# GIN's first layer: where each edge's row goes, ranked in two passes over the source bins, and 17 instead of 14 turns of row scatters inside the GIN stage

## The chip, the cores and the metric

The kernel runs on one core of one Trainium2 chip. The metric is the device time of one execution in microseconds; lower is better. The engines are TensorE (PE in the rows, its weight loads PEld), VectorE (DVE), ScalarE (ACT), GpSimd (POOL) and the DMA queues, of which SP is one.

## The reference, cut to what matters

The whole kernel is four graph layers in a row on one graph of 3125 nodes and 53125 edges, each followed by a residual and a normalisation: a GIN, an edge MLP, a GENConv and an interaction layer. Only the GIN's first of four rounds is touched:

```
for l in range(4):
    S = segment_sum(X[src], dst, 3125)
    Z = (1 + eps[l]) * X + S
    h = relu(bn(Z @ W1[l].T + b1[l]))
    h = relu(bn(h @ W2[l].T + b2[l]))
    X = h @ W3[l].T + b3[l]
```

The interaction layer at the end wants the edges sorted by source, where the input has them sorted by destination. So, beside the GIN, the kernel works out for each edge its place in the order by source, and scatters the edge's row of 24 words there in device memory.

## The kernel before, in words

The stages follow each other with a barrier of all engines between them: `prepare`, `adjacency` (the dense 3125 x 3125 count matrix `adj`, in fp16 in SBUF), `gin`, a normalisation, `edge_mlp`, another, `genconv`, `interaction`. A barrier waits for every engine, SP and GpSimd included.

In `gin` the aggregation of a round is a product of `parts` (the node features times W1, split into three bf16 parts, 97 columns) with `adj`, for 25 tiles of nodes (slots) and seven column pieces of at most 450 (`PIECES`), each piece in a PSUM bank of its own (banks 0 to 6). Bank 7 is what is left.

The places are worked out in the first round, between those products. An edge lies at row p and column c of a 125 x 425 table, in order of destination. Its bin h (0 to 24) is its source node divided by 125, `bins` in float32. For each bin h:

- VectorE marks the edges of the bin: `hots(h)`, L663.
- TensorE counts with two matmuls, L847 and L848, into 426 columns: edges of the bin above in the same column, and in the column before.
- ScalarE copies the counts from PSUM: `bin_steps`, L795.
- VectorE runs a scan along the columns, L671, that starts at the end of the bin before, so that the result is the edge's place in the whole order; it then picks out the edges of the bin, L678, into `chosen[h % 2]`.
- GpSimd adds `chosen` to `places_f`, L640.

The first four bins come before everything else of the round, in banks 5 and 6; then follow the small joined weights (L859 to L867), the node features (L883), and the product, with one bin counted in bank 7 after each slot from the fourth on. The remaining 21 bins stand on VectorE behind the bounds and weights of the later rounds (L753 to L762). ScalarE and VectorE copy the finished pieces out (L816, L773) after the last bin has been added. VectorE then turns places into rows (L776 to L780), and SP writes `deg_row` (L615) and `places` (L617), loads the edges' rows (`pay`) and places in sets of four columns, and GpSimd scatters each column with one indirect DMA (L646): `GIN_TURNS` = 14 turns of 8, so 112 of the 425 columns. `gin` ends when SP has seen them all land. The other 313 columns are scattered in `genconv` (L1631): EACH = (53 - GIN_TURNS) // 3 turns of 8 in each of its three rounds, and what is left behind the last. At the head of each such round GpSimd has a reduction (L1636) on which VectorE waits, behind the scatters of the round before.

Of the kernel before, what the change touches and what calls it, by code (L numbers as in the profile page):

```python
# [7 lines left out]
ALU = mybir.AluOpType  # L8
# [42 lines left out]
GIN_TURNS = 14  # L51
EARLY_BINS, FIRST_TILE = 4, 3
# [43 lines left out]
def build(nc, a, out):  # L96
    ctx = ExitStack()
    with ctx, nc.allow_non_contiguous_dma(reason="small columns"):
# [40 lines left out]
        ranks = dict(bins=apart(P, NC), places_f=apart(P, NC), place_i=apart(P, NC, I32), before=apart(P, P, BF16), upto=apart(P, P, BF16))  # L139
# [20 lines left out]
def prepare(G, keep, ranks):  # L160
# [3 lines left out]
    hi, before, rest = (ranks[k] for k in ("bins", "before", "upto"))  # L164
# [16 lines left out]
    raw_s, of_bin = hi.bitcast(I32), w_(P, NC)  # L181
# [9 lines left out]
    with nc.Block() as block:  # L191
# [10 lines left out]
        def _(eng):  # L202
            imprecise = dict(allow_small_or_imprecise_dtypes=True)
            step = Steps(eng, s_p)
            for out, size in ((lo, 0), (up, 1)):
# [5 lines left out]
            eng.memset(ident[:, :], 0.0)  # L211
            eng.memset(rest, 1.0).then_inc(s_const, 1)
# [5 lines left out]
                              pattern=[[1, P]], channel_multiplier=-1)  # L218

            eng.affine_select(out=rest, in_=rest, compare_op=ALU.is_ge, fill=0.0, base=0,  # L220
                              pattern=[[-1, P]], channel_multiplier=1).then_inc(s_const, 1)
# [35 lines left out]
        def _(eng):  # L257
# [40 lines left out]
            eng.tensor_copy(hi, of_bin)  # L298
# [38 lines left out]
def adjacency(G, keep):  # L337
# [3 lines left out]
    nc, sem, work, ps, adj_all, adj, over_d = (  # L341
        G[k] for k in ("nc", "sem", "work", "ps", "adj_all", "adj", "over_d"))
    key_v, low_v, key_c, low_c, over_n, over = (keep[k] for k in (
        "key_v", "low_v", "key_c", "low_c", "over_n", "over"))
    w_ = Words(work, 0, KEPT)
# [4 lines left out]
    code, base_w, low_iota = w_(P, WCOLS, I16), w_(P, NW), w_(P, P * F, BF16)  # L350
    low_wv = w_(P, NW * F, BF16)
    low3 = low_wv.rearrange("p (w v) -> p w v", v=F)
    iota3 = low_iota.rearrange("p (c v) -> p c v", v=F)
    low_x, code_x = w_(P, P, BF16), w_(P, WCOLS, BF16)
    code16, far, one, key_neg = w_(P, WCOLS, F16), [w_(P, WCOLS, F16) for _ in range(2)], w_(P, 1), w_(P, NW)
# [12 lines left out]
    s_low = sem("remainders_turned")  # L368
# [128 lines left out]
def gin(G, ranks):  # L497
# [50 lines left out]
    one_row = Words(G["extra"], 1536)(1, D)  # L548
    blank = T[1][:, zeroed:t_.at]
    X, S = T[1], T[2]  # L550
    bins, places_f, place_i, before, upto = (ranks[k] for k in ("bins", "places_f", "place_i", "before", "upto"))
    r_ = Words(T[2])
    total, steps, chosen = ([r_(P, n) for _ in range(2)] for n in (NC + 1, NC + 1, NC))
    hot = [r_(P, NC + 2, BF16) for _ in range(2)]
    RANK = [(6, 5)[h % 2] if h < EARLY_BINS else 7 for h in range(NT)]
    assert FIRST_TILE + NT - EARLY_BINS < NT
# [17 lines left out]
    def within_group(g, c0, c1):  # L574
# [3 lines left out]
    s_load, s_x_in, s_zero, s_merge, s_v = (sem(n) for n in ("weights_loaded", "x_loaded", "weights_zeroed", "merge_ready",  # L578
                                                             "vector_step"))
# [8 lines left out]
    s_clear, s_hot, s_rank, s_steps, s_scan = (sem(n) for n in (  # L588
        "ranks_cleared", "bin_hot", "bin_counted", "bin_read_out", "bin_scanned"))
# [3 lines left out]
    with nc.Block() as block:  # L593
        @block.sync
        def _(eng):
            eng.dma_start(T[0], a["x"]).then_inc(s_x_in, 16)
# [32 lines left out]
        def _(eng):  # L629
            eng.memset(blank, 0.0).then_inc(s_zero, 1)  # L630
# [5 lines left out]
            for u in range(NT):  # L636
                eng.wait_ge(s_chosen, u + 1)
                if u:
                    eng.wait_ge(s_placed, u)
                eng.tensor_tensor(places_f, places_f, chosen[u % 2], ALU.add).then_inc(s_placed, 1)  # L640
# [9 lines left out]
        def _(eng):  # L650
# [3 lines left out]
            for k in range(2):  # L654
                eng.memset(hot[k][:, 0:1], 0.0)
                eng.memset(hot[k][:, NC + 1:NC + 2], 0.0).then_inc(s_clear, 1)
            eng.memset(total[1][:, NC:NC + 1], 0.0).then_inc(s_clear, 1)

            def hots(h):

                if h >= 2:
                    eng.wait_ge(s_rank, h - 1)
                eng.tensor_scalar(hot[h % 2][:, 1:NC + 1], bins, float(h), None, ALU.is_equal).then_inc(s_hot, 1)  # L663

            def place_bin(h):
                eng.wait_ge(s_steps, h + 1)
                if h:
                    eng.wait_ge(s_chosen, h)
                else:
                    eng.wait_ge(s_clear, 3)  # L670
# [4 lines left out]
                eng.wait_ge(s_scan, h + 1)  # L675
                if h >= 2:
                    eng.wait_ge(s_placed, h - 1)
                eng.scalar_tensor_tensor(chosen[h % 2], bins, float(h), total[h % 2][:, 0:NC], ALU.is_equal,  # L678
                                         ALU.mult).then_inc(s_chosen, 1)

            hots(0)
            hots(1)
            for u in range(EARLY_BINS):
                place_bin(u)
# [20 lines left out]
            eng.scalar_tensor_tensor(abs_b, abs_b, -1.0, abs_b, ALU.mult, ALU.max).then_inc(s_limits, 1)  # L705
            step(eng.tensor_scalar(w1e[:, 3 * GH:4 * GH], w1, eps[:, 0:1], None, ALU.mult))
# [32 lines left out]
            for l in range(GL):  # L739
# [11 lines left out]
                if l == 0:  # L751
                    eng.wait_ge(s_bound, 1)
# [11 lines left out]
                    for u in range(EARLY_BINS, NT):  # L764
                        place_bin(u)
                    eng.wait_ge(s_placed, NT)
                for i, j in enumerate(DVE_P):
# [6 lines left out]
                if l == 0:  # L774
                    whole, part = places_f, place_i.bitcast(F32)
                    step(eng.tensor_scalar(part, whole, 1.0 / EW, 0.5 / EW - 0.5, ALU.mult, ALU.add))  # L776
                    step(eng.tensor_scalar(part, part, MAGIC, -MAGIC, ALU.add, ALU.add))
                    step(eng.scalar_tensor_tensor(whole, part, -float(EW), whole, ALU.mult, ALU.add))
                    step(eng.scalar_tensor_tensor(whole, whole, float(PAIR * PAIRS), part, ALU.mult, ALU.add))
                    eng.tensor_copy(place_i, whole).then_inc(s_places, 1)  # L780
# [9 lines left out]
        def _(eng):  # L790
            def bin_steps(h):
                eng.wait_ge(s_rank, h + 1)
                if h >= 2:
                    eng.wait_ge(s_scan, h - 1)
                eng.activation(steps[h % 2], ps[0:P, RANK[h], 0:NC + 1], ACT.Copy).then_inc(s_steps, 1)  # L795

            for u in range(EARLY_BINS):
                bin_steps(u)
            eng.wait_ge(s_load, 208)
            for l in range(GL):  # L800
# [5 lines left out]
                if l == 0:  # L806
                    for u in range(EARLY_BINS, NT):
                        bin_steps(u)
                    eng.wait_ge(s_placed, NT)
# [26 lines left out]
        def _(eng):  # L836
            def bin_counts(h):
                eng.wait_ge(s_clear, 2)
                eng.wait_ge(s_hot, h + 1)
                for k in range(h):  # L840
                    if RANK[k] == RANK[h]:
                        free = k
# [1729 lines left out]
```

## Time and profile before

| what | us |
|---|---|
| median of three runs | 2290.88 (2289.26 to 2296.27) |
| the profiled execution, own time | 2297.08 |
| its span, first to last instruction | 2295.4 |
| mean granted TensorE clock | 0.781 of full speed |
| PE / PEld / DVE / ACT / POOL busy | 81% / 58% / 60% / 50% / 59% of the span |

All start times are microseconds from the span's start in the one profiled execution. The profiled execution was 6.2 us slower than the median of the three timed ones. Busy shares of the whole span say little here, since each stage has a limit of its own: the stage `gin` is what counts.

### The profile page before, as it was taken

To read this page: it belongs to the slowest core of one execution; us is meant where nothing else is said; L and a number is where in the kernel's file an instruction comes from. 1 tells how busy PE (TensorE), PEld (TensorE's weight loads), DVE (VectorE), ACT (ScalarE), POOL (GpSimd) and SP (SyncE) were. 2 spreads that over 40 slices of the span, in tenths; PEclk is the share of its full clock that TensorE was granted. 3 is DMA by queue.
4 is the path that set the end of the run, shared out by engine and by line. 5 is a ranking of instruction groups with operands and counts; after the bars stand their busy time and mean duration, and the time that the engine had idled before them with its cause. 6 is when DMAs were issued, how large, how long until landed. Compare 5 with 4: busy or idle time off the path is not lost. (4 is left out here: it accounts for less than half of the span.)

```text
span 2295.4 us, 42015 instructions
## 1 busy us (share of the span) xinstructions
PE 1867.0 (81%) x8353; PEld 1331.7 (58%) x8353; DVE 1371.3 (60%) x4158; ACT 1154.8 (50%) x2623; POOL 1361.8 (59%) x1337
## 2 busy tenths in 40 slices
PE   3888578776898989999889989989986667777677
PEld 2666444445788878888555545545564445555454
DVE  6999592224444444444266577567457777777775
ACT  2999112221566666666253073073135666666663
POOL 1000136772677777777147778878727777777771
PEclk9999697877555565555679999999987777777767
DMA  0000101112444444444111111111232222222221
GB/s 12 0 0 0 45 1 19 18 18 64 106 119 117 117 119 121 119 117 119 57 40 18 19 17 17 20 17 18 40 130 64 64 65 65 64 65 65 65 63 37
DMA packets 195684, 128.61 MB, mean 56 GB/s; under 512 B 138365, under 2 KB 177854, under 8 KB 194587
## 3 DMA queue, kind: packets, MB, share of 16 engines
q0 software_dynamic: 40256, 60.21, 12.2%
q1 hardware_dynamic: 151388, 58.11, 10.1%
q10 hardware_dynamic: 3841, 8.16, 1.0%
q8 instruction: 62, 1.02, 0.2%
q14 instruction: 137, 1.12, 0.2%
HBM read 106.83 MB, written 13.34 MB: 52 GB/s over the span
## 5 line engine op out<-in xcount | busy, mean ns | idle before, releaser
L2204 POOL DMA_INDIRECT adj<-h_rows,adj x416 | 395.5, 951 | 155.9 <-issue 76.5
L1255 POOL DMA_INDIRECT work<-p_rows,small x416 | 394.9, 949 | 126.7 <-issue 101.7
L1631 POOL DMA_INDIRECT edge_rows<-pay,small x313 | 383.0, 1224 | 98.1 <-issue 92.8
L2421 PE MATMUL ps<-adj 128*128 128x125 f32 x928 | 210.9, 365 | 157.7 <-DVE adj L2299 154.1
L1439 PE MATMUL ps<-work 128*128 x1024 | 298.4, 445 | 43.4 <-ACT work L1375 40.6
L2421 PEld LDWEIGHTS ps<-adj 128*128 128x128 f32 x928 | 174.4, 259 | 253.5 <-issue 160.3
L1439 PEld LDWEIGHTS ps<-work 128*128 128x128 f32 x1024 | 231.9, 314 | 66.7 <-issue 59.9
L1332 DVE TENSOR_TENSOR work<-ps,work 128x256 f32<-128x256 f32 x256 | 108.7, 425 | 250.3 <-PE ps L1439 140.2
L1450 PE MATMUL ps<-small,work 128*128 128x64 f32 x1024 | 244.2, 392 | 11.2 <-DVE small L1321 8.0
L1450 PEld LDWEIGHTS ps<-small,work 128*128 128x128 f32 x1024 | 239.0, 321 | 21.7 <-DVE small L1321 17.5
L1993 PE MATMUL ps<-adj,work 125*128 (+2 forms) x1008 | 206.0, 361 | 20.5 <-DVE work L1722 20.5
L1993 PE MATMUL ps<-adj,extra 125*128 (+2 forms) x1092 | 214.8, 352 | 0.0
L486 PE MATMUL ps<-work 125*125 125x500 bf16 x628 | 162.8, 402 | 38.6 <-DVE work L417 38.6
L2411 PE MATMUL ps<-adj 112*128 112x256 f32 x464 | 188.5, 498 | 1.0 <-ACT adj L2344 1.0
L2289 DVE SCALAR_TENSOR_TENSOR adj<-adj 128x128 f32<-128x128 f32 x464 | 144.1, 350 | 65.8 <-POOLq L2209 52.9
L1993 PEld LDWEIGHTS ps<-adj,work 125*128 (+1 forms) x1008 | 100.3, 99 | 119.3 <-issue 29.2
L1372 ACT ACTIVATE work<-work 64x256 f32<-64x256 int32 x256 | 128.4, 502 | 76.6 <-DMA work<-edge_attr 52.9
L1993 PEld LDWEIGHTS ps<-adj,extra 125*128 (+1 forms) x1092 | 106.3, 97 | 101.7 <-issue 0.8
L486 PEld LDWEIGHTS ps<-work 125*125 125x125 bf16 x628 | 114.6, 192 | 86.9 <-DVE work L417 62.2
L1383 ACT ACTIVATE work<-work 128x256 f32<-128x256 f32 x256 | 105.8, 413 | 110.5 <-DVE work L1332 105.4
L646 POOL DMA_INDIRECT edge_rows<-pay,small x112 | 133.3, 1190 | 45.6 <-issue 44.7
L417 DVE TENSOR_SCALAR work<-work 125x500 bf16<-125x500 int16 x549 | 153.5, 401 | 0.0
(417 smaller groups left out, 3111.8 us busy)
## 6 DMA issues: line engine op xcount, KB each, us to landing
work<-dst_all SPq DMA_DIRECT2D x256, 64.0 KB
work<-edge_attr SPq DMA_DIRECT2D x256, 64.0 KB
edge_rows<-pay,small POOLq DMA_INDIRECT x425, 2.7
work<-p_rows,small POOLq DMA_INDIRECT x416
adj<-h_rows,adj POOLq DMA_INDIRECT x416
adj<-adj SPq DMA_DIRECT2D x232, 24.0 KB
pay<-edge_pay SPq DMA_DIRECT2D x106, 46.9 KB
adj<-edge_rows ACTq DMA_DIRECT2D x1, 2496.0 KB, 10.0
```

Of the source, the lines that this page charges most:

```text
L417: eng.tensor_scalar(ring[k][v], code, key_v[:, at], None, ALU.is_equal).then_inc(s_code, 1)
L486: eng.matmul(ps[0:P, parity * WG + k, 0:WCOLS], lows[k][:, v, :], ring[k][v], start=v == 0, stop=v == F - 1).then_inc(s_used, 1)
L646: eng.indirect_dma_start(edge_rows[:, :], bass.IndirectOffsetOnAxis(ap=place[:, k:k + 1], axis=0), pay[:, k * ROW:(k + 1) * ROW], None).th ...
L1255: eng.indirect_dma_start(gathered[:, at:at + D], None, p_rows[:, :], bass.IndirectOffsetOnAxis(ap=src_i[:, c:c + 1], axis=0)).then_inc(s_g ...
L1439: ins = eng.matmul(PROD[v % 2][:, k * D:(k + 1) * D], kmat[b][:, k * EW:(k + 1) * EW], qw[:, bass.ds(w * D, D)], start=True, stop=True)
L1450: ins = eng.matmul(SUM[v % 2], rows[v % 2][:, k * D:(k + 1) * D], hot[v % 2][:, k * MW:(k + 1) * MW], start=k == 0, stop=k == PAIR - 1)
L1631: eng.indirect_dma_start(edge_rows[:, :], bass.IndirectOffsetOnAxis(ap=place[:, k:k + 1], axis=0), pay[:, k * ROW:(k + 1) * ROW], None).th ...
L1993: ins = eng.matmul(ps[:, j, 0:cw], part_of(p, s), cols, start=first, stop=last, skip_group_check=True)
L2204: eng.indirect_dma_start(gathered[:, at:at + D], None, h_rows[:, :], bass.IndirectOffsetOnAxis(ap=row3_i[:, c, DST_C:DST_C + 1], axis=0)). ...
L2289: ins = eng.scalar_tensor_tensor(msg[b][:, k * D:(k + 1) * D], soft[b][:, k * D:(k + 1) * D], rows_t[:, bass.ds((c + k) * ROW + RCUT_C, 1) ...
L2411: eng.matmul(PROD[v % DEPTH], attr_t[f % 2], w_f[:, cols], start=True, stop=True).then_inc(s_prod, 1)
L2421: ins = eng.matmul(SUM[v % 2], msg[b][:, k * D:(k + 1) * D], hot[b][:, k * P:(k + 1) * P], start=k == 0, stop=k == PAIR - 1)
```

## The change

- **Two passes.** The ranks are made in two passes over the bins. Pass one: 25 marks, and one matmul each, that adds the count of every column for each bin into one PSUM tile `TOTAL` (25 x 425). VectorE copies it and runs one scan per bin row (all 25 at once); one small matmul gives each bin's start (`BASE`); four more VectorE instructions give offsets, split in a high and a low bf16 part. Pass two: 25 marks again, and three matmuls per bin (counts above in the column, and the two parts of the bin's offset row) straight into a rank in PSUM. The scan per bin and ScalarE's copy are gone; VectorE multiplies mark and rank out of PSUM. `bins` is bf16.
- **Banks and order.** The ranks use banks 5 and 6 in turn, so the product runs over pieces 0 to 4 for all 25 slots first, with the rank of the next slot's bin before each; pieces 5 and 6 follow for all 25 slots after the last bin has been chosen. Five bins (`EARLY`) are placed ahead of the later rounds' bounds and weights, the other twenty behind them. The matmuls of the bounds move behind the first half of the node features.
- **Rows.** VectorE turns places into rows before it copies the pieces out. SP's list is the same: it waits for all copies, writes `deg_row`, then `places`.
- **x.** The load of x moves from the head of `gin` to the head of `adjacency`, whose buffers make room for it.
- **Scatters.** `GIN_TURNS` is 17: 136 columns in `gin`, 289 in `genconv` (EACH is 12).

```diff
-GIN_TURNS = 14
-EARLY_BINS, FIRST_TILE = 4, 3
+GIN_TURNS = 17
...
+            eng.dma_start(T[0], a["x"]).then_inc(s_x_in, 16)
+            eng.wait_ge(s_x_in, 16)
...
             def place_bin(h):
-                eng.wait_ge(s_steps, h + 1)
...
-                eng.tensor_tensor_scan(total[h % 2], steps[h % 2], steps[h % 2], total[1 - h % 2][:, NC:NC + 1],
-                                       ALU.add, ALU.max).then_inc(s_scan, 1)
                 if h + 2 < NT:
-                    hots(h + 2)
...
+                    hots(NT + h + 2)
+                if h >= 3:
+                    eng.wait_ge(s_placed, h - 2)
+                eng.wait_ge(s_rank, h + 1)
+                eng.scalar_tensor_tensor(chosen[h % 3], bins, float(h), RANK[h], ALU.is_equal,
                                          ALU.mult).then_inc(s_chosen, 1)
...
+            for n in range(NT):
+                hots(n)
+            eng.wait_ge(s_count, NT)
+            step(eng.tensor_copy(off, TOTAL))
+            step(eng.tensor_tensor_scan(upto, off, off, 0.0, ALU.add, ALU.max))
...
+            for u in range(NT):
+                eng.wait_ge(s_hot, u + 1)
+                eng.matmul(TOTAL, mark[:, NT - 1 - u:2 * NT - 1 - u], hot[u % 4], start=u == 0,
+                           stop=u == NT - 1).then_inc(s_count, 1)
...
+            def rank(h):
+                eng.wait_ge(s_hot, NT + h + 1)
+                if h >= 2:
+                    eng.wait_ge(s_chosen, h - 1)
+                at = ident16[:, h:h + 1].to_broadcast([NT, P])
+                eng.matmul(RANK[h], before, hot[(NT + h) % 4], start=True, stop=False)
+                eng.matmul(RANK[h], at, off_high, start=False, stop=False)
+                eng.matmul(RANK[h], at, off_low, start=False, stop=True).then_inc(s_rank, 1)
...
+                    eng.wait_ge(s_off, 1)
+                    rank(0)
+                    for slot in range(NT):
+                        if slot + 1 < NT:
+                            rank(slot + 1)
+                        tile(slot, PIECES[0:5])
+                    eng.wait_ge(s_chosen, NT)
+                    for slot in range(NT):
+                        tile(slot, PIECES[5:])
```

## Rows read from the trace of the kernel before

**Rows 1.** Windows of the product with ranks: busy by engine (count), clock, DMA.

```profile
277.70:344.90 67.20, 48.47 (x219) 28.14 (x219) 61.43 (x115) 11.09 (x22) 19.72 (x21) 0.95 0.00 0
```

**Rows 2.** Timeline, end of GIN: start, duration, engine, line, operation, count [idle before].

```profile
513.64 0.54 DVE L786 TENSOR_SCALAR work<-ps,small 128x312 f32<-128x312 f32 x1 [0.72 <-PE ps L973]
...
522.51 1.19 POOL L646 DMA_INDIRECT edge_rows<-pay,small  x1 [0.30 <-issue]
526.94 1.28 ACT L1052 ACT_TABLE_LOAD   x1 [13.20 <-PEq L111]
```

**Rows 3.** The scatters' line in GIN: durations min/median/max, first and last start.

```profile
L646 POOL DMA_INDIRECT edge_rows<-pay,small x112: 1182/1187/1517, 356.6 to 522.5; - x112
```

**Rows 4.** Timeline of one of the 21 bins between products.

```profile
308.79 0.34 PE L848 MATMUL ps<-work,extra 125*125 125x426 bf16 x1
308.97 1.49 PE L907 MATMUL ps<-adj,work 125*97 125x450 f16 x7
309.07 0.94 POOL L640 TENSOR_TENSOR extra<-extra,work 125x425 f32<-125x425 f32 x1 [1.76 <-DVE work L678]
309.10 1.82 DVE L671 TENSOR_TENSOR_SCAN work<-work 125x426 f32<-125x426 f32 x1
...
310.83 0.35 DVE L663 TENSOR_SCALAR work<-extra 125x425 bf16<-125x425 f32 x1
311.11 0.59 DVE L678 SCALAR_TENSOR_TENSOR work<-extra,work 125x425 f32<-125x425 f32 x1
```

**Rows 5.** Timeline, from GIN's start to the product.

```profile
241.94 1.48 POOL L630 MEMSET work<- 128x1664 f32 x1 [196.95 <-POOLq L111]
...
242.59 1.53 DVE L663 TENSOR_SCALAR work<-extra 125x425 bf16<-125x425 f32 x2
...
257.53 0.64 PE L859 MATMUL ps<-work 128*128 128x32 f32 x2 [7.08 <-DVE work L691]
...
264.97 10.71 PE L883 MATMUL ps<-small,work 128*125 128x32 f32 x50
...
277.74 2.81 PE L907 MATMUL ps<-adj,work 125*97 125x450 f16 x7 [2.06 <-DVE work L749]
```

**Rows 6.** Timeline: first and last of the 52 instructions of bounds and weights.

```profile
277.52 0.25 DVE L753 TENSOR_SCALAR small<-ps 128x96 f32<-128x96 f32 x1
...
286.94 0.16 DVE L761 MEMSET work<- 32x125 f32 x1
```

**Rows 7.** Windows at the product's start, columns as in rows 1.

```profile
280.00:285.00 5.00, 5.00 (x23) 2.96 (x21) 4.74 (x32) 0.00 (x0) 0.00 (x0) 0.86 0.00 0
285.00:290.00 5.00, 2.98 (x12) 1.86 (x12) 3.89 (x17) 0.53 (x1) 0.00 (x0) 0.82 0.00 0
```

**Rows 8.** The line of a VectorE operation of this kind out of PSUM.

```profile
L1756 DVE SCALAR_TENSOR_TENSOR ps<-ps,work x42: 599/625/635, 1276.7 to 1655.1; 128x450 f32<-128x450 f32 x36, 128x425 f32<-128x425 f32 x6
```

**Rows 9.** Timeline: VectorE reads PSUM while GpSimd clears a tile.

```profile
1172.58 3.67 DVE L1681 TENSOR_SCALAR work<-ps 125x512 f32<-125x512 f32 x6
...
1174.17 2.70 POOL L1645 MEMSET work<- 128x3125 bf16 x1
```

**Rows 10.** Timeline, from the last product's copies to the first scatter.

```profile
344.85 2.20 DVE L773 COPY work<-ps 97x450 f32<-97x450 f32 x4 [1.05 <-POOL extra L640]
...
349.47 0.29 SPq L617 DMA_DIRECT2D places<-extra  x1
...
356.60 1.52 POOL L646 DMA_INDIRECT edge_rows<-pay,small  x1 [11.78 <-issue]
```

**Rows 11.** Timeline of GENConv: last round's reduction, and the stage's end.

```profile
1512.19 0.37 POOL L1636 PARTITION_ALL_REDUCE small<-small  x1 [6.57 <-DVE small L1677]
...
1676.56 1.19 POOL L1631 DMA_INDIRECT edge_rows<-pay,small  x1 [0.31 <-issue]
...
1677.82 0.53 ACT L1951 ACTIVATE work<-ps 128x425 f32<-128x425 f32 x1 [0.93 <-PE ps L2042]
1680.58 0.38 SPq L2063 DMA_DIRECT2D adj<-int_w_in  x1
```

More of the change, by code:

```diff
@@ L138, in build @@
         apart = Words(extra)
-        ranks = dict(bins=apart(P, NC), places_f=apart(P, NC), place_i=apart(P, NC, I32), before=apart(P, P, BF16), upto=apart(P, P, BF16))
+        ranks = dict(sources=apart(P, NC, I32), bins=apart(P, NC, BF16), places_f=apart(P, NC), place_i=apart(P, NC, I32),
+                     before=apart(P, P, BF16), one_row=apart(1, D), mark=apart(P, 2 * NT - 1, BF16),
+                     ident16=apart(NT, NT, BF16), before_f=apart(NT, NT), off_low=apart(NT, NC, BF16),
+                     off_high=Words(extra)(NT, NC, BF16))
         phase(prepare, keep, ranks)
@@ L163, in prepare @@
     key_v, low_v, key_c, low_c, over_n = (keep[k] for k in ("key_v", "low_v", "key_c", "low_c", "over_n"))
-    hi, before, rest = (ranks[k] for k in ("bins", "before", "upto"))
+    raw_s, bins, before = (ranks[k] for k in ("sources", "bins", "before"))
     over_d = G["over_d"]
@@ L297, in _ @@
             floor_div(of_bin, of_bin, P)
-            eng.tensor_copy(hi, of_bin)
+            eng.tensor_copy(bins, of_bin)
             eng.wait_ge(s_keym, 1)
@@ L547, in gin @@
     merge = [t_(D, WIDE) for _ in range(GL)]
-    one_row = Words(G["extra"], 1536)(1, D)
     blank = T[1][:, zeroed:t_.at]
     X, S = T[1], T[2]
-    bins, places_f, place_i, before, upto = (ranks[k] for k in ("bins", "places_f", "place_i", "before", "upto"))
+    bins, places_f, place_i, before, one_row, mark, ident16, before_f = (
+        ranks[k] for k in ("bins", "places_f", "place_i", "before", "one_row", "mark", "ident16", "before_f"))
     r_ = Words(T[2])
[L553 to L556, printed above, removed]
+    chosen, hot = [r_(P, NC) for _ in range(3)], [r_(P, NC, BF16) for _ in range(4)]
+    upto, off, base = r_(NT, NC), r_(NT, NC), r_(NT, 1)
+    off_high, off_low = ranks["off_high"], ranks["off_low"]
+    TOTAL, BASE = ps[0:NT, 5, 0:NC], ps[0:NT, 6, 0:1]
+    RANK = [ps[0:P, 5 + h % 2, 0:NC] for h in range(NT)]
+    EARLY = 5
     JOIN, ROWS, OWN = (ps[:, 7, 0:(GL - 1) * GH], ps[0:1, 7, 128:128 + (GL - 1) * GH],
@@ L629, in _ @@
         def _(eng):
+            eng.memset(mark, 0.0).then_inc(s_mark, 1)
+            eng.wait_ge(s_mark, 1)
+            eng.memset(mark[:, NT - 1:NT], 1.0).then_inc(s_mark, 1)
             eng.memset(blank, 0.0).then_inc(s_zero, 1)
@@ L681, in _, with hots @@
[L681 to L684, printed above, removed]
+            eng.tensor_copy(ident16, ident[0:NT, 0:NT])
+            eng.tensor_copy(before_f, before[0:NT, 0:NT])
+            def hots(n):
+                if n >= 4:
+                    if n - 4 < NT:
+                        eng.wait_ge(s_count, n - 3)
+                    else:
+                        eng.wait_ge(s_rank, n - 4 - NT + 1)
+                eng.tensor_scalar(hot[n % 4], bins, float(n % NT), None, ALU.is_equal).then_inc(s_hot, 1)
@@ L751, in _ @@
                 if l == 0:
+                    for u in range(EARLY):
+                        place_bin(u)
                     eng.wait_ge(s_bound, 1)
@@ L885, in _ @@
                         ins.then_inc(s_y, 1)
+                        if b == 0:
+                            eng.wait_ge(s_scan, 1)
+                            eng.matmul(BASE, before_f, upto[:, NC - 1:NC], start=True, stop=True).then_inc(s_base, 1)
+                            bounds()
                 else:
```

139 lines of the change are left out of this document (45 added, 94 removed).

## The prediction

> **What bounds the kernel now.** I read the list of stages first (windows by engine), then the timeline of the stage `gin` from both ends. The change lies inside one stage, and stages are parted by barriers, so what counts is what ends `gin` last, and what ends `genconv` last, since scatters move between the two.
>
> The end of `gin` is GpSimd's. VectorE's last instruction ends at 514.18, ScalarE then idles 13.20 us, and the next stage begins at 526.94; the last scatter starts at 522.51 [rows 2]. So what ends the stage is the chain: last scatter's start + 4.43 us (its issue, landing, SP's wait, the barrier). The 112 scatters are evenly spaced: (522.51 - 356.60) / 111 = 1.495 us each [rows 2, 3], with nothing waited for. The compute of the stage is done some 12 us before it would be missed.
>
> The first scatter is set by the ranks. From 277.7 to 344.9 VectorE is busy 61.4 of 67.2 us at a clock of 0.95 [rows 1]: each bin costs a scan of 1.82 (beside GpSimd's add of 0.94, which holds it up), a mark, 0.35, and a pick, 0.59; some 2.70 us from bin to bin (309.10 to the next scan) [rows 4]. TensorE waits for it in every bin. From the first copy of the pieces to the first scatter are 356.60 - 344.85 = 11.75 us; from `places` to the first scatter, two queue trips, 7.13 [rows 10].
>
> **The change part by part.** I follow the new chain in the stage.
>
> *x early.* The product of x, L883, starts at 264.97, 23 us after the stage began, and behind other TensorE work [rows 5]. Its load was hidden; moving it is worth 0 here, and in `adjacency` it lies beside some 200 us without transfers. The weights, next on SP's queue, come earlier too; nobody waited for them. If something in `adjacency` were held up, it would be by the load's few us at its head: 0 to 5, I take 0.
>
> *Pass one.* Before, the joined weights (L859) begin at 257.53 after four bins of 2.70, 10.8 us [rows 4, 5]. Now 25 marks and 25 matmuls of 425 columns come first. At the low clock seven of 450 took 2.81, 0.38 for 425 columns [rows 5], so 25 take 9.5. Then a copy (0.6, as rows 8), and one scan of 1.1 to 1.8 (the upper end: [rows 4]). The merge copies that follow no longer run beside GpSimd's adds. The first mark is held up by GpSimd's clearing as before (two marks took 1.53 rather than 0.70 beside a memset of 1.48 [rows 4, 5]), and some more of it, since now 25 marks meet all the clearing. I take 1 us earlier, 256.5, within 3 us either way.
>
> *Up to the product.* From L859's start to L883's, 264.97 - 257.53 = 7.4, included 1.0 in which TensorE waited for VectorE's limits; with the bounds moved behind 16 of 25 feature tiles that wait has cover. 256.5 + 6.4 + 10.7 (L883) + 0.3 (`BASE`) = 273.9; the product began 2.1 after L883's end (264.97 + 10.71 to 277.74) [rows 5]: 276.0 now, 1.7 earlier. The offsets' five VectorE instructions (2.5 us) have the bounds and the other nine tiles as cover (6 us).
>
> *The product.* A slot is now 3 rank matmuls and 5 pieces. At the full clock seven pieces take 1.49, of which 0.34 is one matmul's whole way [rows 4]: 0.19 each, so 8 x 0.19 = 1.52 a slot. Windows: the clock was 0.86 in 280 to 285 and 0.82 in 285 to 290, after a pause of 2 us [rows 7]; each start costs about 3.5 us at half rate, 1.8 us of time. First run: ranks 0 to 6 and slots 0 to 5, 7 x 3 + 6 x 5 = 51 matmuls, 9.7 + 1.8 = 11.5, to 287.5. Rank 7 must wait for bin 5 to be chosen. Bin 4 is chosen at 276.0 + 30 x 0.19 + 1.8 + 0.6 = 284.1; then VectorE has the bounds and weights, 286.94 + 0.3 - 277.52 = 9.8 us [rows 6], to 293.9, then bin 5, 0.35 + 0.60 [rows 4, 8]: 294.8. TensorE stands for 7.3 us. This is the new stall: the old code had it too, but with 1.2 us idle in each bin to lose it in. Second run: 18 ranks and 19 slots, 149 matmuls, 28.3 + 1.8, to 324.9. Then pieces 5 and 6, 50 matmuls, 9.4: 334.3, against copies from 344.85 before.
>
> Does VectorE or GpSimd bound a bin instead? Mark 0.35, pick 0.60 [rows 4, 8] and add 0.94 [rows 4] lie between 0.95 (beside each other) and 1.89 (one after the other), against TensorE's 1.52. The row nearest in kind is a VectorE operation out of PSUM beside GpSimd: six of 512 columns took 3.67, 0.61 each, with a memset of 2.70 inside [rows 9]; they did not wait. I take the mark and the add as excluding each other, the pick as free: 1.29, and TensorE binds.
>
> The Trainium skill's SBUF — State Buffer, section Who interferes with whom, says a VectorE instruction with two SBUF inputs contends with a GpSimd instruction that reads SBUF, and one with at most one SBUF input outside the two-port modes does not. By that the removed scan waited and the new pick, out of PSUM, does not; the trace agrees for the scan (1.82 beside the add). Without the rule, at 1.89 a bin, the sum would be 6.7 us higher, the rival below.
>
> *To the first scatter.* Rows are made of places before the copies, behind the second set of products (9.4 us of cover against about 2.5). But SP still waits for all seven copies before `deg_row` and `places`. Pieces 5 and 6, two of the four copies of 2.20 [rows 10]: 334.3 + 1.2 = 335.5, `places` at 335.9, first scatter 7.13 later: 343.0, 13.6 earlier than before.
>
> *The scatters.* 136 of them: the last starts at 343.0 + 135 x 1.495 = 544.8, and the next stage at + 4.43 = 549.3, against 526.94: **+22.3**. 24 scatters are 35.9 us more and the start only gives 13.6 back. The compute ends about 13 us earlier too (z starts with every copy ready at 335.5), near 501, so the gain there is behind GpSimd and worth nothing.
>
> *GENConv.* It has 24 scatters less, eight in each round. In round 3 GpSimd had waited 6.57 us for VectorE before its reduction, so scatters do not hold the rounds [rows 11]; only the stage's end is near: last scatter starts 1676.56, last compute ends 1678.35, next stage 1680.58 [rows 11]. With 12 us less on GpSimd the compute ends it; 1.0 us for a barrier leaves 1679.4: **-1.2**. Its bounds are 0 and 1680.58 - 1678.35 = 2.2, if scatters do not slow VectorE; a further 3 us if each of 24 did by 0.1.
>
> Sum: +22.3 - 1.2 = **+21.1**. On the profiled execution, 2297.08 + 21.1 = 2318.2; on the median, 6.2 lower, **2312**.
>
> **The rivals.**
> - *GENConv gives it back* (the other sign). If the rounds there moved with GpSimd's scatters, the 24 would return 35.9: 22.3 - 35.9 = -13.6, 2277. Against it stands the 6.57 us wait of GpSimd for VectorE [rows 11]. It decides from 22.3 returned; between 15.4 and 29.2 the change would measure as none.
> - *No stall, quick clock.* If TensorE stays at the full clock and the weights fit beside the first bins: -7.3 - 3.5 from the product, -2 before it: +8.3, 2299. For it: all of pass one is dense TensorE work just before. Even here GpSimd ends the stage last.
> - *Mark, pick and add in a row.* 1.89 a bin for 18 bins is 18 x 0.37 = +6.7: 2318.7. For it: the scan's 1.82 [rows 4].
> - *The clock stays low.* 199 matmuls at double: +38, 2350. Against it: 0.95 in [rows 1] at less TensorE work.
>
> **How the numbers follow.** Forecast 0.60 (2304 to 2317), no stall 0.13, one after the other 0.15, clock 0.03, GENConv giving back all 0.04, giving back part so that nothing is left 0.05. Range 2299 to 2325: it takes in the quick case and the port case with start up to 5 us later, and leaves out 0.03 + 0.04 + 0.05 and tails. 0.3% is 6.9 us, about what a measurement tells from no change. Faster 0.04; within 0.07 (0.05 and the quick edge of the quick case); slower 0.89.
>
> **What would show it.** Idle of all engines but GpSimd at the end of `gin` near 48 us (before 13.20); first scatter L646 near 343 with 136 at 1.495; a pause of TensorE of some 7 us after rank 6; slots 1.5 us apart after it; in GENConv longer waits of GpSimd for VectorE and an end set by ScalarE's last copy. It is wrong if the first scatter starts before 329, if scatters come faster than 1.495, or if `genconv` is shorter by more than 5 us.

## The result, and the profile after

The changed kernel took 2348.95 us (2347.44 to 2353.70, four runs) against 2290.07 (2286.93 to 2296.27, four runs) of the kernel before on the same chip: ratio 1.0257, 95% interval 1.0241 to 1.0272. I had forecast 2312, 21 us slower, with a range from 2299 to 2325. It is 59 us slower: the direction was right, the size was not, and the time is that of the rival to which I gave 0.03, the clock that stays low. The profiled execution has a span of 2345.6 us and a mean clock of 0.762 (before 2295.4 and 0.781). One run among those of the experiments below, at 5133.91 us far out of line with the other four of its kernel, stands in no median.

I read the stage `gin` in the same order as before. The windows of the product with ranks, which answer to [rows 1, 7] (columns as there); the second fence is the timeline of one slot in it, which answers to [rows 4].

```profile
276.50:287.50 11.00, 11.00 (x28) 4.58 (x27) 3.13 (x8) 0.00 (x0) 4.03 (x4) 0.50 0.00 0
287.50:300.00 12.50, 9.11 (x23) 3.61 (x21) 11.18 (x58) 0.00 (x0) 0.96 (x2) 0.50 0.00 1
...
310.00:320.00 10.00, 10.00 (x26) 4.11 (x24) 2.35 (x6) 0.00 (x0) 2.96 (x3) 0.50 0.00 0
...
358.00:365.00 7.00, 7.00 (x31) 4.31 (x30) 3.63 (x8) 1.64 (x3) 1.08 (x1) 0.78 0.01 2
365.00:370.00 5.00, 5.00 (x29) 3.34 (x28) 0.00 (x0) 0.00 (x0) 0.00 (x0) 1.00 0.00 0
```

```profile
308.04 2.11 PE L903 MATMUL ps<-adj,work 125*97 125x450 f16 x5
308.21 0.60 DVE L675 SCALAR_TENSOR_TENSOR work<-extra,ps 125x425 f32<-125x425 bf16 x1 [2.51 <-PE ps L848]
...
309.94 0.56 PE L846 MATMUL ps<-work,extra 125*125 125x425 bf16 x1
310.43 0.18 PEld L847 LDWEIGHTS ps<-extra 25*125 25x125 bf16 x1 [0.64 <-issue]
310.44 0.61 PE L847 MATMUL ps<-extra 25*125 25x425 bf16 x1
...
310.84 0.56 PE L848 MATMUL ps<-extra 25*125 25x425 bf16 x1
311.33 0.25 PEld L903 LDWEIGHTS ps<-adj,work 125*97 125x97 bf16 x2 [0.61 <-issue]
```

The reader is to see three things. TensorE is now busy 10.00 of 10.00 us, where it had been busy 48.47 of 67.20 [rows 1], and yet the granted clock is 0.50, 1.2 GHz, from the first rank to the last, where it had been 0.95. It rises to 1.00 (2.4 GHz) in 358 to 365, when the ranks are over (the last one's matmuls start at 356.05 to 356.95) and the pieces are left, whose matmuls all contract over 125 rows. And a slot, from 308.04 to 311.33, takes 3.29 us, not 1.52: twice 1.52 and 0.25 more, since wherever the height changes between 125 and 25 rows the weight load waits 0.6 us for nothing shown and the next matmul starts 0.49 to 0.50 after the one before, not 0.35 to 0.40. VectorE waits 2.51 us of each slot for the rank.

The stage from its start to the first scatter (timeline; answers to [rows 5, 6, 10]):

```profile
244.00 0.14 POOL L630 MEMSET extra<- 125x49 bf16 x1 [197.09 <-POOLq L110]
...
246.02 7.54 PE L838 MATMUL ps<-work,extra 125*25 125x425 bf16 x25 [3.96 <-DVE work L667]
...
254.21 1.03 DVE L682 TENSOR_TENSOR_SCAN work<-work 25x425 f32<-25x425 f32 x1
...
275.18 0.58 PE L846 MATMUL ps<-work,extra 125*125 125x425 bf16 x1 [2.17 <-DVE work L667]
...
288.60 0.25 DVE L762 TENSOR_SCALAR small<-ps 128x96 f32<-128x96 f32 x1
...
300.04 0.58 PE L846 MATMUL ps<-work,extra 125*125 125x425 bf16 x1 [3.44 <-DVE work L675]
...
370.49 1.13 DVE L788 COPY work<-ps 97x450 f32<-97x450 f32 x2 [7.53 <-PE ps L903]
...
372.00 0.29 SPq L617 DMA_DIRECT2D places<-extra  x1
...
379.27 1.52 POOL L649 DMA_INDIRECT edge_rows<-pay,small  x1 [19.90 <-issue]
```

The end of the stage (timeline, answers to [rows 2]), and the scatters' line (to [rows 3]):

```profile
538.74 0.54 DVE L794 TENSOR_SCALAR work<-ps,small 128x312 f32<-128x312 f32 x1 [0.72 <-PE ps L970]
...
581.37 1.19 POOL L649 DMA_INDIRECT edge_rows<-pay,small  x1 [0.30 <-issue]
585.47 1.28 ACT L1049 ACT_TABLE_LOAD   x1 [46.63 <-PEq L110]
```

```profile
L649 POOL DMA_INDIRECT edge_rows<-pay,small x136: 1182/1187/1517, 379.3 to 581.4; - x136
```

So GpSimd ends the stage, as before, and everything else waits 46.6 us for it. The stage ends at 585.47 against 526.94: +58.5, as much as the medians differ (the two profiles differ by 50.2 only, since behind GIN the profiled execution took 8.3 less, see the last part). It has two parts: 24 scatters more, (581.37 - 379.27) / 135 = 1.497 us each, +35.9; and a first scatter at 379.27 instead of 356.60 [rows 10], +22.7 (the parts are off by rounding and the last landing), where I had forecast 343.0, 13.6 earlier.

In GENConv the last round's reduction now waits 20.04 us for VectorE, where it had waited 6.57 [rows 11], and ScalarE's copies, not a scatter, end the stage (timeline):

```profile
1568.15 0.36 POOL L1633 PARTITION_ALL_REDUCE small<-small  x1 [20.04 <-DVE small L1674]
...
1733.93 0.53 ACT L1948 ACTIVATE work<-ps 128x425 f32<-128x425 f32 x1 [0.93 <-PE ps L2039]
1735.76 0.38 SPq L2060 DMA_DIRECT2D adj<-int_w_in  x1
```

### The profile page after: what moved, and what is told of

Same layout as the page of the kernel before. It is cut to its first block and busy times, and to the rows that moved or that the text cites. A ratio compares the mean times of both kernels' runs of the same rounds, so it can differ in the third digit from the quotient of the medians.

```text
span 2345.6 us, 42050 instructions
## 1 busy us (share of the span) xinstructions
PE 1914.9 (82%) x8405; PEld 1352.9 (58%) x8405; DVE 1338.5 (57%) x4162; ACT 1142.8 (49%) x2598; POOL 1360.1 (58%) x1337
## 5 line engine op out<-in xcount | busy, mean ns | idle before, releaser
L1436 PE MATMUL ps<-work 128*128 x1024 | 307.4, 456 | 31.9 <-ACT work L1372 29.3
L1436 PEld LDWEIGHTS ps<-work 128*128 128x128 f32 x1024 | 239.3, 324 | 54.3 <-issue 48.1
L1447 PE MATMUL ps<-small,work 128*128 128x64 f32 x1024 | 251.1, 401 | 9.5 <-DVE small L1318 7.9
L1447 PEld LDWEIGHTS ps<-small,work 128*128 128x128 f32 x1024 | 245.8, 330 | 20.5 <-DVE small L1318 18.5
L1990 PE MATMUL ps<-adj,work 125*128 (+2 forms) x1008 | 205.8, 361 | 21.4 <-DVE work L1719 21.4
L486 PE MATMUL ps<-work 125*125 125x500 bf16 x628 | 164.0, 405 | 39.5 <-DVE work L417 38.5
```

Of the source, the lines that this page charges most:

```text
L486: eng.matmul(ps[0:P, parity * WG + k, 0:WCOLS], lows[k][:, v, :], ring[k][v], start=v == 0, stop=v == F - 1).then_inc(s_used, 1)
L1436: ins = eng.matmul(PROD[v % 2][:, k * D:(k + 1) * D], kmat[b][:, k * EW:(k + 1) * EW], qw[:, bass.ds(w * D, D)], start=True, stop=True)
L1447: ins = eng.matmul(SUM[v % 2], rows[v % 2][:, k * D:(k + 1) * D], hot[v % 2][:, k * MW:(k + 1) * MW], start=k == 0, stop=k == PAIR - 1)
L1990: ins = eng.matmul(ps[:, j, 0:cw], part_of(p, s), cols, start=first, stop=last, skip_group_check=True)
```

## The experiments

Ratios are to the kernel before, run on the same chip in turn with it, with their 95% intervals. What was tested first: theory A, the two matmuls of a bin that contract over 25 rows hold the clock down; theory B, the clock stays down because it was down when the ranks began.

### 14 turns of scatters as before, the rest of the change kept

```diff
-GIN_TURNS = 17
+GIN_TURNS = 14
```

> The changed kernel with 14 instead of 17 turns of scatters in GIN, nothing else. If the 24 moved scatters cost what their spacing says, GIN is 24 x 1.495 = 35.9 us shorter (last scatter near 379.3 + 111 x 1.495 = 545.2, next stage near 549.5 instead of 585.5) and GENConv gives back the 1 to 3 us it had gained: 2348.95 - 33 to -35 = 2314 to 2316. A rival: GENConv's rounds wait for scatters, then up to 36 us come back there and the whole is no faster than 2340.

2318.01 us (2315.97 to 2321.20), ratio 1.0106 (1.0089 to 1.0122). The scatters run from 379.8 to 545.8. The end of the stage, timeline:

```profile
550.26 1.28 ACT L1049 ACT_TABLE_LOAD   x1 [10.82 <-PEq L110]
```

The 24 scatters account for 35.2 us of the stage's end (585.47 - 550.26), and by the ratios for (1.0257 - 1.0106) x 2292 = 34.6 of the 59. The other 24 us come from the ranks: their two passes, at this clock, are slower than what they replace.

### The offset matmuls over 125 rows, 100 of them zero

```diff
-                     ident16=apart(NT, NT, BF16), before_f=apart(NT, NT), off_low=apart(NT, NC, BF16),
-                     off_high=Words(extra)(NT, NC, BF16))
+                     ident16=apart(P, NT, BF16), before_f=apart(NT, NT), off_low=apart(P, NC, BF16),
+                     off_high=Words(extra)(P, NC, BF16))
...
-            eng.tensor_copy(ident16, ident[0:NT, 0:NT])
+            eng.memset(off_high, 0.0)
+            step(eng.memset(off_low, 0.0))
+            eng.tensor_copy(ident16, ident[0:P, 0:NT])
...
-                at = ident16[:, h:h + 1].to_broadcast([NT, P])
+                at = ident16[:, h:h + 1].to_broadcast([P, P])
```

> 14 turns, and the two offset matmuls of each rank contract over 125 rows instead of 25 (the other 100 rows are zeros in both operands): the same ranks, the same number of columns. Theory A, the 25-row matmuls in the mix keep the clock at its low level: the clock rises within some us of the product's start, a slot falls from 3.29 to some 1.55 us, the first scatter comes some 30 us earlier than 379 and the time is near 2285. Theory B, the clock rises only in an unbroken run of pieces and then stays up: nothing changes but the gaps at the change of height (about 0.3 us a slot at the low clock), so 2306 to 2316.

2279.57 us (2278.44 to 2282.28), ratio 0.9937 (0.9921 to 0.9954): 38 us less than the kernel with 14 turns, and less than the kernel before. Windows (columns as in rows 1), and the timeline of a slot's matmuls:

```profile
276.00:290.00 14.00, 10.95 (x51) 6.96 (x49) 9.81 (x39) 0.00 (x0) 4.97 (x5) 0.87 0.00 1
290.00:300.00 10.00, 4.94 (x15) 3.03 (x16) 7.10 (x34) 0.00 (x0) 2.95 (x3) 0.53 0.00 1
300.00:324.00 24.00, 24.00 (x130) 16.43 (x128) 12.00 (x30) 0.00 (x0) 15.71 (x16) 1.00 0.00 1
```

```profile
309.26 0.34 PE L848 MATMUL ps<-work,extra 125*125 125x425 bf16 x1
...
310.76 0.34 PE L848 MATMUL ps<-work,extra 125*125 125x425 bf16 x1
```

Multiplying 100 more rows of zeros changes no result and no count of matmuls, and it brings the clock to 1.00 and a slot to 1.50 us, my 1.52. The pause after rank 6 is there too: 8.11 us, TensorE waiting for VectorE. The clock falls in it to 0.50, as 290 to 300 show (0.53), and with ranks and pieces in the same mix it is back at 1.00 from 300. So it is the height of the two matmuls that decides whether the clock comes up, as theory A has it. The first scatter starts at 343.1.

### Three slots of pieces before the first rank

```diff
-                    rank(0)
                     for slot in range(NT):
-                        if slot + 1 < NT:
-                            rank(slot + 1)
+                        if slot == 3:
+                            rank(0)
+                        if slot >= 3:
+                            rank(slot - 3 + 1)
                         tile(slot, PIECES[0:5])
+                    for u in range(NT - 3 + 1, NT):
+                        rank(u)
```

> 14 turns, and three slots of five pieces each run before the first rank, as the kernel before had it (ranks 23 and 24 follow the last slot); the offset matmuls stay at 25 rows. Theory B: the clock rises in the head start and stays up, slots of 1.55 us, time near 2287. Theory A: it rises and falls back once ranks are in the mix, or never rises: 2312 to 2318. Both: VectorE's first pick is later by three slots, 3 to 6 us.

2313.96 us (2313.11 to 2319.36), ratio 1.0091 (1.0074 to 1.0108). Windows:

```profile
276.00:290.00 14.00, 14.00 (x58) 6.92 (x56) 6.50 (x15) 0.00 (x0) 4.97 (x5) 0.88 0.00 1
280.00:290.00 10.00, 10.00 (x46) 4.83 (x45) 6.50 (x15) 0.00 (x0) 4.97 (x5) 1.00 0.00 1
290.00:300.00 10.00, 2.54 (x10) 1.01 (x8) 9.24 (x53) 0.00 (x0) 1.12 (x2) 0.65 0.00 1
300.00:355.00 55.00, 54.42 (x132) 22.39 (x131) 13.44 (x33) 0.00 (x0) 17.54 (x18) 0.50 0.00 0
```

and the timeline, one 25-row matmul before the pause, and the first matmul behind it:

```profile
286.15 0.39 PE L847 MATMUL ps<-extra 25*125 25x425 bf16 x1
...
298.80 0.59 PE L846 MATMUL ps<-work,extra 125*125 125x425 bf16 x1 [7.46 <-DVE work L675]
```

The head start does bring the clock up (0.88 in the first window), and it stays at 1.00 from 280 to 290 with 25-row ranks among the pieces, two matmuls of eight as before; slots took 1.77 us there. It falls in the pause for VectorE's weights, with TensorE idle for 7.46 us, and does not come back in 55 us with TensorE busy for 54.42 of them and the same mix running. So neither theory stands as I had put it. The mix did not pull the clock down in the eleven us or so that it ran at 1.00, which speaks against theory A's "falls back once ranks are in the mix"; but from 0.50 it did not raise it, while the 125-row mix of the second experiment, behind a pause as long, did, which theory B alone does not explain. It takes both: a low clock when the mix begins, and the 25 rows. Whether the 25-row mix would keep the clock for all of the ranks, if no pause cut them in two, was not tried.

### x loaded in GIN again, and the places sent before the last copies

```diff
-            eng.dma_start(T[0], a["x"]).then_inc(s_x_in, 16)
-            eng.wait_ge(s_x_in, 16)
...
+            eng.dma_start(T[0], a["x"]).then_inc(s_x_in, 16)
             for dst, src in ((w1, a["gin_w1"]), (w1r,
...
+            eng.wait_ge(s_places, 1)
+            eng.dma_start(places[:, :], place_i).then_inc(s_saved, 16)
+            eng.wait_ge(s_saved, 16)
+            for b in SETS:
+                fill(0, b)
             eng.wait_ge(s_sa, len(ACT_P))
             eng.wait_ge(s_sv, len(DVE_P))
             eng.dma_start(G["deg_row"][:, :], S[3 * GH:3 * GH + 1, :]).then_inc(s_deg, 16)
-            eng.wait_ge(s_places, 1)
-            eng.dma_start(places[:, :], place_i).then_inc(s_saved, 16)
```

> 14 turns, the load of x back at the head of GIN, and SP writes the places and fills the first sets before it waits for the copies and writes the degrees. Two separate places in the trace. x: GpSimd's first instruction in the adjacency stage comes back from 44.4 to 42.5 and GIN begins 1.9 us earlier; a rival is that these 1.9 us were chance, then nothing moves. Places: they are ready 10 us before the last copy, so the first scatter is 7.1 us after them, at 369 minus 1.9 instead of 379.3. GIN's end is then the later of scatters (367.2 + 166 + 4 = 537) and compute (539 + 1.2 - 1.9): 2314 - 11 = 2303.

2302.89 us (2301.31 to 2304.80, four runs), ratio 1.0038 (1.0022 to 1.0054), 15.1 us less than with 14 turns alone. The scatters run from 367.6 instead of 379.8, and the compute now ends the stage (ScalarE idle 1.47 before the next). Part of it is x. GpSimd's first instruction of `adjacency`, timeline of the kernel before (first fence) and after (second); in this one it starts at 43.00:

```profile
42.49 0.54 POOL L389 IOTA work<- 125x500 int16 x1 [24.53 <-issue]
```

```profile
36.02 0.36 SPq L383 DMA_DIRECT2D work<-x  x1
44.41 0.54 POOL L389 IOTA work<- 125x500 int16 x1 [26.43 <-issue]
```

In the nine profiles with x early it starts at 44.18 to 45.14; in the five with x in GIN (the kernel before among them) at 42.49 to 43.08. The stage has no other slack there: GIN begins 1.2 to 2.6 us later for it. What GpSimd waits for at that place the trace does not show.

### The change itself, 17 turns, with the offset matmuls over 125 rows

The edit of the second experiment, `GIN_TURNS` left at 17.

> The change as it is, 17 turns, with one thing altered: the two matmuls that add a bin's offset contract over 125 rows, of which 100 are zero, in place of 25. This is the kernel that my prediction took the changed one to be. If the prediction's sum was right but for the clock: the clock is 1.00 from about 300 on, the first scatter starts near 343.0, the last at 544.8, the next stage at 549.3, and the time is 21 us over the kernel before: ratio 1.009. If the 17 turns cost more than their 35.9 us, or GENConv gives more back than in the run with 14 turns, the ratio lies outside 1.0075 to 1.0110.

2313.44 us (2309.25 to 2313.75) against 2292.28, ratio 1.0089 (1.0073 to 1.0104): 21.2 us slower than before. Timeline:

```profile
342.95 1.52 POOL L649 DMA_INDIRECT edge_rows<-pay,small  x1 [17.89 <-issue]
...
545.00 1.19 POOL L649 DMA_INDIRECT edge_rows<-pay,small  x1 [0.30 <-issue]
549.10 1.28 ACT L1051 ACT_TABLE_LOAD   x1 [48.30 <-PEq L110]
```

This is the kernel that the prediction described: forecast 343.0, 544.8, 549.3 and +21.1. That the times agree to 0.1 us is luck, since the interval reaches from 16.7 to 23.8; the three places in the trace agree to 0.2.

### Over 64 rows, and one of the two over 125

The first takes 64 rows where the second experiment takes 125 (`ident16`, `off_low` and `off_high` of 64 rows); the other keeps `off_high` at 25 rows and gives only `off_low` 125:

```diff
-                eng.matmul(RANK[h], at, off_low, start=False, stop=True).then_inc(s_rank, 1)
+                eng.matmul(RANK[h], tall, off_low, start=False, stop=True).then_inc(s_rank, 1)
```

> 14 turns; the two offset matmuls contract over 64 rows (39 of them zero) instead of 25 or 125. If what keeps the clock at 0.50 is the change of the contraction's height between matmuls and the gap at the weight load that comes with it (0.49 rather than 0.35 us from start to start), the height of 64 brings the same gaps: clock 0.50 to about 360, first scatter near 379, ratio about 1.011. If it is how much of the array the slot fills on the mean, 64 rows lie well toward the full height (mean of 8 matmuls 110 of 125 rows instead of 100), and the clock is 1.00 for at least part of the run: first scatter between 343 and 360, ratio 0.994 to 1.001. I lean to the second, at 0.6.

> 14 turns; of the two offset matmuls the first keeps its 25 rows, the second contracts over 125 (100 of them zero). The eight matmuls of a slot then fill 112 of 125 rows on the mean, about as with 64 rows for both (110, where the clock was 1.00), but one of the eight still has only 25. If the clock goes by how much of the array is filled on the mean, it is 1.00 from some point on: first scatter near 348, ratio 0.998. If a matmul over 25 rows is itself what holds it, the clock is 0.50 to about 360: first scatter near 378, ratio 1.010. I lean to the first, at 0.8.

64 rows: 2288.34 us (2283.90 to 2296.49, ten runs), ratio 0.9987 (0.9974 to 1.0000). One of two: 2290.89 (2281.66 to 2296.38, ten runs), ratio 0.9994 (0.9979 to 1.0009). Windows of the first, then of the second, and the second's timeline:

```profile
300.00:310.00 10.00, 10.00 (x44) 4.60 (x42) 3.92 (x10) 0.00 (x0) 4.52 (x6) 0.92 0.00 0
310.00:320.00 10.00, 10.00 (x47) 4.97 (x47) 4.39 (x11) 0.00 (x0) 5.49 (x6) 1.00 0.01 2
```

```profile
310.00:320.00 10.00, 10.00 (x46) 5.22 (x45) 4.39 (x12) 0.00 (x0) 5.70 (x6) 1.00 0.00 0
```

```profile
303.25 0.34 PE L848 MATMUL ps<-work,extra 125*125 125x425 bf16 x1
303.52 0.39 PE L849 MATMUL ps<-extra 25*125 25x425 bf16 x1
303.84 0.39 PE L850 MATMUL ps<-extra 125*125 125x425 bf16 x1
...
305.03 0.34 PE L848 MATMUL ps<-work,extra 125*125 125x425 bf16 x1
```

In both the clock comes up to 1.00. So neither the gaps at a change of height (they are all there: 0.27, 0.32 and 0.23 from start to start, a slot of 1.77 to 1.78 us, not 1.50) nor the mere presence of a 25-row matmul is what kept it down; two of eight at 25 rows did, one of eight at 25 or two at 64 did not, though both mixes began again behind the pause at a low clock too (0.60 and 0.56 in 290 to 300). Both runs went the way to which I leaned. The gaps have a price of their own: some 0.28 us a slot at this clock, with a first scatter at 350.1 and 350.7 against 343.1.

### Both again, for the spread of their times

> The kernel with one of the two offset matmuls over 125 rows, again, for another profile. Its ten times went from 2281.7 to 2296.4, median 2290.9, and the profile was of the fastest, with the clock at 0.89 in 300 to 310 and 1.00 after it. If the point at which the clock rises varies from execution to execution where the mix still has short matmuls, this profile has its time near 2291, a clock of 0.5 for some 10 us or more after 300 and a first scatter near 360. If the clock has no part in the variation, the clock after 300 is as before whatever the time.

> The kernel with both offset matmuls over 64 rows, again, for another profile: its ten times went from 2283.9 to 2296.5, median 2288.3, and the profiled one took 2286.6 with the clock at 0.92 in 300 to 310. The same two readings as for the one before: a time that differs by x from 2286.6 has its first scatter later by x than 350.1 and x of low clock more after 300, or the difference lies elsewhere.

Timed once each, on another chip: 2290.31 and 2299.38 us. The clock's part in the spread, which I had suspected, is 1.5 us at most: in 300 to 310 it was 0.93 and 0.81 (before 0.89 and 0.92), 1.00 from 310 in both, and the first scatter came at 350.1 and 351.6. The execution of 2299.38 was 12.8 us longer than the first profile of that kernel but only 1.3 of it lies in GIN (its end at 521.89 against 520.63). GENConv began 8.1 later (1165.52 against 1157.47) and ended 13.2 later. So these medians say less of the ranks than the stage's end does.

### All three together, with 14 turns

The edits of the second and fourth experiments.

> 14 turns, offset matmuls over 125 rows, x loaded in GIN again, and the places written and the first columns loaded before the last copies and deg_row. With the clock full the last two pieces take only 9.3 us after the places are made, so moving the places ahead gains that and the first copy, 8 us, and the load of x moved back some 1.2 to 1.9: first scatter near 333.5, last near 499.7, scatters' end at 504.1, about where the compute ends (501.1 + 1.4, some 1.5 earlier): next stage near 504, 9.6 us before that of the kernel with the tall matmuls alone. Time 2270, ratio 0.990. If the load of x is worth nothing and the places gain only the queue's trip for deg_row, 2275.

2273.02 us (2270.47 to 2277.43), ratio 0.9907 (0.9894 to 0.9921). The scatters run from 333.5 to 500.1 and the next stage begins at 504.50, as worked out.

### One matmul for both parts of an offset

```diff
-            eng.scalar_tensor_tensor(off_low[0:NT, :], off_high[0:NT, :], -1.0, off, ALU.mult, ALU.add)
+            eng.scalar_tensor_tensor(off_high[32:32 + NT, :], off_high[0:NT, :], -1.0, off, ALU.mult, ALU.add)
...
-                eng.matmul(RANK[h], at, off_high, start=False, stop=False)
-                eng.matmul(RANK[h], at, off_low, start=False, stop=True).then_inc(s_rank, 1)
+                eng.matmul(RANK[h], at, off_high, start=False, stop=True).then_inc(s_rank, 1)
```

> As the one before, and both parts of the offset in one matmul (the low part in rows 32 to 56 of the same tile): two matmuls a rank in place of three. If TensorE sets a bin's pace, 25 matmuls at 0.19 less are 4.7 us off both the first scatter and the compute behind it, less what the stall takes back: 2266, ratio 0.988. If GpSimd's add with VectorE's mark and pick sets it, the bins still come every 1.3 us or so and nothing is gained: 2270.

2268.64 us (2262.62 to 2270.91), ratio 0.9884 (0.9865 to 0.9903). A bin takes 1.33 us. Timeline of one, with the next bin's start:

```profile
306.08 0.60 DVE L677 SCALAR_TENSOR_TENSOR work<-extra,ps 125x425 f32<-125x425 bf16 x1 [0.54 <-PE ps L849]
...
306.76 0.94 POOL L643 TENSOR_TENSOR extra<-extra,work 125x425 f32<-125x425 f32 x1 [0.39 <-DVE work L677]
...
307.40 0.60 DVE L677 SCALAR_TENSOR_TENSOR work<-extra,ps 125x425 f32<-125x425 bf16 x1 [0.53 <-PE ps L849]
```

VectorE still waits 0.5 us for TensorE in each bin, and its pick at 307.40 runs in 0.60 beside the add that ends at 307.70. The first scatter comes at 330.7, 2.7 us earlier, of the 4.7 expected; the stage's end is 3.4 earlier.

### VectorE's bounds and weights in pieces between the bins

```diff
+                    for u in range(EARLY, NT):
+                        next(work_list, None)
+                        place_bin(u)
```

`work_list` is the block of bounds and weights, cut into 18 pieces.

> As the kernel with one offset matmul (2269, ratio 0.988), and VectorE's 52 instructions of bounds and weights cut into 18 pieces of about 0.55 us, one ahead of each later bin. If TensorE's pause between 276 and 300 (8.5 us idle there, clock 0.54 in its second half) is the price of those instructions standing in one block, most of it goes: a bin costs VectorE 0.27 + 0.60 + 0.55 = 1.42 against TensorE's 1.33, first scatter near 324, GIN shorter by 6 to 7 us at both its scatters and its compute: 2262, ratio 0.985. If the semaphores between the pieces make each longer than 0.55, so that VectorE sets the pace at 1.7 a bin, as much is lost as is won: 2269.

2267.43 us (2266.45 to 2269.03), ratio 0.9889 (0.9870 to 0.9909): no gain over the last. Windows (290 to 320 as one), and the timeline of one bin:

```profile
290.00:320.00 30.00, 22.07 (x105) 12.05 (x103) 28.78 (x71) 0.00 (x0) 14.77 (x16) 1.00 0.00 1
```

```profile
301.35 0.60 DVE L677 SCALAR_TENSOR_TENSOR work<-extra,ps 125x425 f32<-125x425 bf16 x1
...
302.02 0.94 POOL L643 TENSOR_TENSOR extra<-extra,work 125x425 f32<-125x425 f32 x1 [1.21 <-DVE work L677]
...
302.09 0.92 DVE L741 SCALAR_TENSOR_TENSOR work<-ident,small 32x32 f32<-32x32 f32 x1
```

The long pause is gone, but VectorE sets the pace, 2.15 us from pick to pick (301.35 to 303.50). A piece costs more here than its 0.55 in the block: the instruction with two inputs in SBUF takes 0.92 beside GpSimd's add, 0.17 in the block without it. The Trainium skill's SBUF — State Buffer, section Who interferes with whom, has such an instruction contend with a GpSimd instruction that reads SBUF; this trace agrees, and with the other half of the rule, for the pick out of PSUM. The windows show something else: TensorE is idle 26% of the time here and keeps its clock of 1.00.

## Why the prediction was right in direction and wrong in size

**The step that failed** is the product: "At the full clock seven pieces take 1.49 ... 8 x 0.19 = 1.52 a slot", with "about 3.5 us at half rate" a start. I took it that the clock, low at each start, would come up after some 3.5 us of busy TensorE whatever the matmuls are, and counted a 25-row matmul like any other. Its rival, "199 matmuls at double: +38, 2350", was dismissed with [rows 1], the 0.95 "at less TensorE work". That row was of matmuls that all contracted over 125 rows; it said nothing of a mix in which a quarter does not. That is where 0.03 was unearned: the diff showed a form of matmul that no row had at issue. What the runs showed: started at a low clock with 25 rows in two of eight, 0.50 throughout and 2349; with 125 rows, 1.00 from 300 on and 2313.

The rival's price was near for reasons that in part cancel. The product and its pause ended 36.9 us later than forecast (9.9 - 3.9 + 30.9, below), against its 38. It left out the gaps at a change of height (0.25 a slot, some 6 us) and the shorter pause (-3.9), and it charged twice for the 3.6 us of low clock at the two starts. And none of the signs of being wrong that I had named (a first scatter before 329, quicker scatters, a shorter GENConv) came up: they all stood for a time below the forecast. What did show the miss were the signs of being right: first scatter, slots and pause were not as foretold.

The Trainium skill's TensorE: Matmul & The Clock Gate, section What's actually happening, says that the default state is throttled and that activity releases the throttle. The traces agree for the fall (0.53 in 290 to 300 of the second experiment, around its pause of 8.11 us), and for the rise only if activity is more than being busy: 10.00 of 10.00 us busy stayed at 0.50 here, and 22.07 of 30.00 held 1.00 in the last experiment.

**Point by point**, with the measured first scatter 36.3 us after the forecast one (379.27 against 343.0):

- *Stage start.* x early "is worth 0" and costs up to 5 in `adjacency`: it cost 2.1 (GIN from 244.00 instead of 241.94).
- *Pass one and up to the product.* Forecast start 276.0, measured 275.18, 0.8 earlier. Two misses cancel in it: the 2.1 above, and 2.9 gained, since the 25 count matmuls took 7.54 (I had 9.5, at the low clock throughout; it was 0.77 in 250 to 254) and the scan of 25 rows 1.03, below the lower end of its bounds.
- *First run.* 11.5 us forecast, 21.4 measured (275.18 to 300.04 less the pause): +9.9.
- *The pause.* 7.3 forecast, 3.44 measured, -3.9: the slower first run covered more of VectorE's block (288.60 to 299.08, 10.5 us; I had 9.8, where my own terms give 9.7). At the full clock it is 8.11.
- *Second run and the last pieces.* 294.8 to 334.3, 39.5 us forecast; about 300.0 to 370.4, 70.4 measured: +30.9.
- *To the first scatter.* 8.7 forecast, 8.9 measured.
- These add up to 36.3: -0.8 + 9.9 - 3.9 + 30.9 + 0.2.
- *The scatters.* 35.9 forecast, 35.9 measured; last start + 4.43 forecast, 4.10 measured.
- *Mark, pick and add.* "The pick as free, 1.29" is borne out: bins of 1.33 run with VectorE waiting. One after the other, 1.89, is refuted.
- *GENConv.* Forecast -1.2. From its own start (1222.67 after, 1167.35 before) to its end it took 513.1 against 513.2. That it gives the scatters back is refuted: GpSimd's waits grew from 6.57 to 20.04 instead. The 3.2 us by which the stages between GIN and GENConv were shorter, and the 5.0 after GENConv, lie where nothing was changed, and within what the same kernel varies there (636.8 and 643.6 us for the first stretch in the two profiles with 64 rows, 609.5 and 615.3 for the second in the two with one of two over 125).
- *Sum.* With the clock restored and nothing else, 21.2 against the forecast 21.1. A slip of counting had no weight in it: 51 and 149 matmuls are 200, not 199.

What stays open is why, behind the pause, two matmuls of 25 rows in eight hold the clock down and one does not. Heights between were not tried one by one, and I draw no bound from three points. Nor is a mix of full height always at 1.00: in `edge_mlp`, which this change does not touch and whose matmuls there are float32 over 128 rows, the clock is 0.55 and 0.52 in 600 to 800 of the kernel before with TensorE busy 91.05 and 90.42 of 100 us. I did not study it.

## What to carry to other kernels

Before a stall on another engine is taken away so that TensorE can run without a pause, look at the shape of what will run: here the denser stream began at half the clock and stayed there, since a quarter of its matmuls contracted over 25 rows. The same mix ran at the full clock where one that contracted over 125 rows throughout had brought it up, until the next pause. Padding the contraction with zeros to the height of the neighbours took no more matmuls and gave 38 us. And work that moves out of a stage with slack into the one that its engine ends is paid in full: 24 scatters were 35 us here and gave nothing back in GENConv; with the turns as before, the padded matmuls, one offset matmul, the places sent first and x left where it was, the same idea is 1.2% faster than the kernel before.

## What the runs showed of the hardware that I had not expected

- The granted clock stayed at 0.50 for some 80 us with TensorE busy all the time (276.5 to 358), less one pause of 3.44 us, and was 1.00 with TensorE idle 26% of the time.
- One and the same mix of heights ran at 1.00 from 280 to 290 and at 0.50 from 300 to 355, in one execution, with a pause of 7.46 us between (the third experiment).
- A change of the contraction's height from one matmul to the next costs a gap at the weight load: starts 0.49 apart instead of 0.35 at 1.2 GHz, 0.27 instead of 0.18 at 2.4 GHz.
- Loading x at the head of `adjacency`, whose issue takes 0.36 us on SP's queue, put off GpSimd's first instruction there by 1.1 to 2.7 us, in every profile.
